# A cross-interaction tower on one core: layer-1 slices cut by samples, G in the same chunk without the DRAM trip, and the weights turned in another order

## The reference

```python
e = jnp.stack([tbl_0[ids[:, 0]], ..., tbl_38[ids[:, 38]]], axis=1)      # (1024, 39, 16)
def _cin_layer(X0, Xi, W, b):
    Wr = W.reshape(H, F0_, Fi)
    return jnp.einsum('hjk,bjd,bkd->bhd', Wr, X0, Xi) + b[None, :, None]
X0 = embedded_features
Xi = X0
for W, b in Ws:                       # three layers
    Xi = _cin_layer(X0, Xi, W, b)
    res.append(Xi.sum(axis=2))        # z0, z1, z2: 128 numbers a sample each
h = jnp.concatenate([z, dense_ctx], axis=1)
h = jnp.maximum(h @ W_top1 + b_top1, 0.0)
h = jnp.maximum(h @ W_top2 + b_top2, 0.0)
y = h @ W_top3
```

## Time and profile before

| what | us |
|---|---|
| median of three runs | 1378.81 |
| lowest and highest run | 1375.5, 1385.89 |
| span of the profiled execution | 1393.5 |
| first layer-1 matmul starts at | 125.98 |
| step 7 of layer 1 starts at | 1209.68 |
| layer 1 ends about | 1354.2 |

### The profile page before, as it was taken

The page is one execution under the profiler, slowest core; times in us unless marked ns, Lnnn a source line. Parts: engine busy times, 40 slices in busy tenths (PEclk is TensorE's granted clock), DMA queues, the critical chain, the costliest instruction groups (busy, mean ns, idle before and its releaser), DMA issues.

```text
span 1393.5 us, 23236 instructions
## 1 busy us (share of the span) xinstructions
PE 1272.0 (91%) x6037; PEld 1041.9 (75%) x6037; DVE 1087.9 (78%) x2694; ACT 1039.8 (75%) x3353; POOL 882.6 (63%) x654
## 2 busy tenths in 40 slices
PE   2127999999999999999999999999999999999997
PEld 2115778777888878787887878787888888887876
DVE  3125898988888788888888888888888888988992
ACT  1114888888788887788777877888778887788772
POOL 6572777786776867686776877686776745363000
PEclk7556999999999999999999999999999999999999
DMA  4042522242233221242223221242232221240000
GB/s 147 10 107 56 139 63 62 75 99 52 62 75 89 57 58 48 68 100 52 65 72 82 57 67 48 68 96 56 56 81 78 58 64 46 65 98 25 16 16 16
DMA packets 71598, 92.39 MB, mean 66 GB/s; under 512 B 31745, under 2 KB 53762, under 8 KB 70306
## 3 DMA queue, kind: packets, MB, share of 16 engines
q1 hardware_dynamic: 61318, 87.75, 24.5%
q0 software_dynamic: 9984, 2.58, 2.0%
q10 hardware_dynamic: 156, 0.48, 0.1%
HBM read 21.03 MB, written 10.95 MB: 23 GB/s over the span
## 4 chain that ended last, share of the span: by engine, by line
PE 81%; DVE 5%; ACT 4%; another core or an unknown queue 4%; issue 4%; DMA 1%; ACTq 0%; POOL 0%; DVEq 0%; SPq 0%; POOLq 0%
PE ring L1098 19%; PE ring L1100 19%; PE ring L1099 18%; PE side L998 4%; PE side L1065 4%; PE l_ps L984 4%; PE l_ps L986 3%; PE l_ps L985 3%; ACT terms L692 2%; DVE x_s L852 2%; DVE terms L897 2%; PE side L1017 1%; PE side L1048 1%; PE side L1026 1%
## 5 line engine op out<-in xcount | busy, mean ns | idle before, releaser
L692 ACT ACTIVATE terms<-ring,e_both 128x128 f32<-128x128 f32 x2944 | 839.2, 403 | 214.4 <-PE ring L1100 180.2
L1098 PE MATMUL ring<-w_hi,x_hi 128*128 128x512 f32 (+1 forms) x1280 | 556.5, 435 | 15.8 <-ACT terms L692 8.7
L897 DVE SCALAR_TENSOR_TENSOR terms<-ring,e_both,terms 128x128 f32<-128x128 f32 x1792 | 507.9, 344 | 65.2 <-PE ring L1100 57.3
L1100 PE MATMUL ring<-w_hi,x_lo 128*128 128x512 f32 (+1 forms) x1280 | 499.1, 390 | 0.0
L1099 PE MATMUL ring<-w_lo,x_hi 128*128 128x512 f32 (+1 forms) x1280 | 497.2, 388 | 0.0
L852 DVE TENSOR_REDUCE x_s<-terms 128x32 f32<-128x800 f32 x512 | 489.1, 976 | 0.7 <-ACT terms L692 0.7
L500 POOL TENSOR_TENSOR pairs_lo<-pairs,pairs_hi 117x1024 fp32r<-117x1024 f32 (+1 forms) x104 | 250.1, 2404 | 231.7 <-ACT pairs_hi L603 226.7
L458 POOL DMA_INDIRECT e_in<-in_tbl,idx x312 | 302.1, 968 | 93.8 <-issue 70.6
L1098 PEld LDWEIGHTS ring<-w_hi,x_hi 128*128 128x128 f32 x1280 | 242.9, 190 | 74.4 <-ACT terms L692 17.7
L1100 PEld LDWEIGHTS ring<-w_hi,x_lo 128*128 128x128 f32 x1280 | 241.1, 188 | 50.5
L489 POOL TENSOR_TENSOR pairs<-x_rep,pairs 117x1024 f32<-117x1024 f32 (+1 forms) x104 | 250.3, 2406 | 36.4 <-DMA pairs<-x_t 35.4
(11 more groups left out here) (113 smaller groups left out, 655.8 us busy)
## 6 DMA issues: line engine op xcount, KB each, us to landing
pairs<-x_t SPq DMA_DIRECT2D x312, 156.0 KB
x_scratch<-x_s SPq DMA_DIRECT2D x32, 256.0 KB, 2.2
x_r<-x_scratch SPq DMA_DIRECT2D x7, 1024.0 KB
x_rep<-x_t SPq DMA_DIRECT2D x45, 156.0 KB
e_in<-in_tbl,idx POOLq DMA_INDIRECT x312
x_scratch<-e_both SPq DMA_DIRECT2D x8, 312.0 KB, 7.6
g_t<-in_L_rec_W SPq DMA_DIRECT2D x1, 2496.0 KB, 15.9
xb<-x_scratch SPq DMA_DIRECT2D x8, 312.0 KB
```

Source lines behind the costliest of these rows:

```text
L692: last = nc.scalar.activation(term(d, ACT_BEFORE[d][g] + i), twos(ring[:, (GROUPS * d + g) % RING, i * H:(i + 1) * H]), ACT.Copy, scale=sc ...
L897: nc.vector.scalar_tensor_tensor(out=acc, in0=y, scalar=scale_of(j, d), in1=acc, op0=ALU.mult, op1=ALU.add).then_inc(dve_unit, 1)
L1098: nc.tensor.matmul(acc, x1_hi[:, x], w1_hi[:, w], start=True, stop=False)
L1100: nc.tensor.matmul(acc, x1_lo[:, x], w1_hi[:, w], start=False, stop=True).then_inc(y_group, 1)
```

## The change

A layer-1 slice now is 8 samples with their 16 columns. It is what a G matmul needs, so `sum_terms` writes a slice of x2 straight to `x2_r` and G of slice r runs in the same step, at the new `G_AT`, without DRAM. For this `x0_t` and x1 have sample-major columns (ScalarE writes `x0_t` with a stride of 16 elements), `x0_t` has two slots (partitions 0 and 64 up), and the scales come from `xb`, X0 by samples and columns, which is written to DRAM and read back a chunk ahead in two slots. All G of a chunk use one bank, so each waits for the evacuation of the one before. z2, the network's three layers and y of a chunk all run in the next step, slices 2 to 9, where g_t is free before its next G. `copy_x0`, the two halves of z0 with their add on GpSimd, and the x2 DMAs are gone. `move_x0` is one turning copy at (2, 5); X0's four transposes follow one at a time through one bank.

In the setup six batches of W1 are turned before step -1 (`W1_EARLY`). The other four and all of W2, which is loaded at the start into `terms`, are turned at (6, 0) of step -1, behind X0's transposes. In step -1 33 gathers for chunk 1 follow (`INDEX_SLICE` 4), and VectorE makes the product of the next tile before the rest of the last.

```diff
-    X0T_AT, X0T_OUT_AT, X0T_BANK = ((5, 0), (5, 2), (8, 9), (9, 9)), ((5, 3), (5, 5), (9, 3), (10, 3)), (1, 0, 1, 1)
+    X0T_AT, X0T_OUT_AT = ((3, 2), (3, 7), (4, 2), (4, 7)), ((3, 5), (4, 0), (4, 5), (5, 0))
+    Z2_PLACES = [(d, g) for d in range(2, 6) for g in range(GROUPS)][1:1 + FIELDS]
+    G_AT = ((6, 5), (6, 9), (7, 2), (7, 7), (8, 2), (8, 7), (9, 2), (9, 7), (10, 4), (11, 4), (12, 4), (13, 4), (14, 4),
+            (15, 4), (16, 4), (17, 4))
+    BLOCK_AT = [d - 1 for d, g in G_AT]
+    H1_AT, H1_OUT_AT = ((6, 6), (6, 8), (7, 4), (7, 5)), (7, 8)
+    H2_AT, H2_OUT_AT = ((8, 3), (8, 4)), (8, 8)
+    Y_AT, Y_OUT_AT = (9, 3), (9, 6)
...
-    GATHERS = (3, 3, 2, 2, 0, 2, 4, 2, 3, 2, 3, 2, 3, 2, 4, 2)
-    INDEX_SLICE = 5
+    GATHERS = (3, 3, 0, 0, 2, 2, 5, 2, 2, 2, 3, 2, 3, 2, 5, 3)
+    INDEX_SLICE = 4
...
+    W1_PIECE, W1_FIRST, W1_EARLY = 2, 2, 6
+    W1_REST_AT = (6, 0)
...
-            return e_mid[:, j, d:d + 1] if d < CUR_FROM else e_cur[:, d, j:j + 1]
+            return xb[:, odd, d, j:j + 1]
...
+            sp.dma_start(w2_raw, W2).then_inc(w2_in, 16)
...
+                    nc.scalar.activation(
+                        x0_t(1 - odd).rearrange("p (b d) -> p d b", d=D)[:, 4 * q:4 * q + 4, :],
+                        side[0:WRAPPED, 0, :].rearrange("p (d b) -> p d b", d=4),
+                        ACT.Copy).then_inc(x0t_ready, 1)
...
+                    nc.vector.tensor_reduce(z0[:, odd, n * half:n * (half + 1)],
+                                            l0_ps[:, :].rearrange("p (b d) -> p b d", d=D),
+                                            AX.X, ALU.add).then_inc(z0_summed, 1)
...
-                        twos(x2_s[:, d % X2_SLOTS, h]),
+                        twos(x2_r[:, d, h]),
...
+                def slice_g(chunk, r):
+
+                    n = SLICES * chunk + r
+                    after(pe, block_made, n + 1)
+                    after(pe, x2_done, n + 1)
+                    after(pe, g_ready, n)
+                    if r == 0:
+                        after(pe, z2_ready, chunk)
+                    nc.tensor.matmul(side[:, 1, 0:SAMPLES * GCOLS], x2_r[:, r, :],
+                                     blocks[:, r % BLOCK_SLOTS, :, :].rearrange("p b j -> p (b j)"),
+                                     start=True, stop=True).then_inc(g_ps, 1)
...
+                    if not layer1 and (d, g) == W1_REST_AT:
+                        for q in range(W1_EARLY, GROUPS):
+                            w1_turned(q)
+                        for q in range(GROUPS):
+                            w2_turned(q)
```

More of the change, by code:

```diff
@@ new lines, in step @@
+                        if not layer1 and i == FIRST_SLOTS - 1:
+                            x0_write()
+                        if i == (0 if layer1 else FIRST_SLOTS):
+                            xb_back()
+                    rep(c + 1, 1, 1 - odd)
+                    pair_tile(c + 1, PAIR_TILES, 1 - odd)
+                if layer1 and not following:
+                    after(sp, dense_ps, c)
+                    sp.dma_start(dense_raw[:, :], dense_ctx[c * P:(c + 1) * P, :]).then_inc(dense_in, 16)
@@ L450, in _ @@
             sp.wait_ge(y_out, 32)
-            for i in range(2):
-                sp.wait_ge(x2_out[i], 32 * CHUNKS)
             sp.wait_ge(x0_out, 16 * CHUNKS)
@@ L470, in _, with step @@
                 gather(0, f)
-            def step(c, odd, layer1, following, previous, mlp, gathers):
+            def step(c, odd, layer1, following, previous, gathers):
                 def next_index():
@@ L564, in _, with step @@
                 last.then_inc(setup_hi, 1)
-            for q in range(W1_FIRST, GROUPS):
+            for q in range(W1_FIRST, W1_EARLY):
                 w1_upper(q)
-            def step(c, odd, layer1, following, previous, mlp, gathers):
+            def step(c, odd, layer1, following, previous, gathers):
                 def x1_half(chunk, half):
@@ new lines, in first_lower @@
+                def first_lower(d):
+                    chunk, i = tile_made(c, d, layer1, following)
+                    n = TILES * chunk + i
+                    rows = ROWS_OF[TILE[i][1]]
+                    after(dve, pair_hi, n + 1)
+                    after(dve, pair_used, n - 1)
+                    nc.vector.tensor_tensor(pairs_lo[0:rows, i % 2, :], pair_slot(chunk, i)[0][0:rows, :],
+                                            pairs_hi[0:rows, i % 2, :].bitcast(f32),
+                                            ALU.subtract).then_inc(pair_lo, 1)
@@ new lines, in first_pairs @@
+                def first_pairs(d, g):
+                    if (d, g) == W1_REST_AT:
+                        for q in range(W1_EARLY, GROUPS):
+                            w1_lower(q)
+                    if g == MADE_MID and tile_made(c, d, layer1, following) and d < D - 1:
+                        first_product(d)
+                        if d > FIRST_MADE:
+                            first_lower(d - 1)
+                    if (d, g) == (FIRST_MADE + PAIR_TILES, 0):
+                        first_lower(d - 1)
+                    if (d, g) == (D - 1, 8):
+                        first_product(d)
+                    if (d, g) == (D - 1, 9):
+                        first_lower(d)
@@ L864, in side_work @@
                             z0_half(half)
-                    if not layer1:
+                    if not layer1 and following:
                         first_pairs(d, g)
@@ L1001, in side_work @@
                             last.then_inc(z2_ps, 1)
+                    if following and (d, g) in X0T_AT:
+                        q = X0T_AT.index((d, g))
+                        if q == 0:
+                            after(pe, e_ready, c + 2)
+                            after(pe, y_ready, c - 1)
+                        else:
+                            after(pe, x0t_ready, 4 * (c + 1) + q)
+                        for i in range(4):
+                            last = nc.tensor.transpose(side[0:TURNED, 0, i * P:(i + 1) * P],
+                                                       e_df[:, 4 * q + i, :], ident[:, :])
+                        last.then_inc(x0t_ps, 1)
                     if previous and (d, g) == DENSE_AT:
```

582 lines of the change are left out of this document (213 added, 369 removed).

## The result

| what | before, us | after, us |
|---|---|---|
| median of the timed runs | 1380.57 (4 runs, 1375.5 to 1385.89) | 1422.74 (4 runs, 1419.8 to 1427.33) |
| span of the profiled execution | 1393.5 | 1420.8 |
| first layer-1 matmul starts | 125.98 | 140.71 |
| eight steps of layer 1 | 1228.2 | 1256.3 |
| from there to the end | 39.3 | 23.8 |

The ratio is 1.0279, with a 95% interval of 1.0224 to 1.0335: the change makes the kernel slower by about 42 us. The forecast was 1365 with a range of 1342 to 1386, so it was wrong in size and in sign.

What follows compares the result with a forecast made beforehand. TensorE's work was taken to bound the middle steps, chains of waits the start and tail. Tail -17.6, layer 1 -2 and start +6 gave -13.6, so 1378.8 became 1365 us, range 1342 to 1386.

Steps and rivals of the forecast that it cites:

- tail -17.6: After the last layer-1 step: z2 no longer waits for x2 from DRAM and starts 17.6 us earlier.
- layer 1 -2: Eight layer-1 steps: steps 2 to 5 save 4 together, step 1 pays +1.7, steps 0 and 7 nothing; together -2 us.
- start +6: Up to the first layer-1 matmul: W1 and W2 batches come late under the gathers, so it starts at 132, +6 us.
- bound of -14: Tail's smallest gain: -14 us if TensorE is half clocked after its 2 us without work.
- Rival D: Tail: the DRAM trip was not what it waited for; tail -12, sum -8, 1371 us; chance 0.10.
- bounds of -10 to +10: Layer 1: -10 us if all waits go but 3.5 us, +10 if light slices 10 to 14 wait for GpSimd.
- rival B: Slices 6 to 9: single bank makes G wait for the evacuation before, +36 us, sum +22, 1401; chance 0.12.
- X0's four parts take 8.6 and are there at 65: Start: X0's transposes and ScalarE's writes, begun at 56.2, take 8.6 us and finish at 65, not late.
- outer bound: Start at its worst: no batch gets through the gathers and X0's parts are late too; first layer-1 matmul at 140, +14 us.
- The sum: Whole kernel: -13.6 us against the profiled span, 1393.5 to about 1379.9; carried to the median, 1365.
- rival A: Start: TensorE's signals are not late under the second run of gathers; start -14 to -18, 1345 us; chance 0.15.
- C: Start eats the tail: X0's parts late and step 0 pays for its G; sum -3, 1376 us; chance 0.13.

Runs made afterwards that it cites:

- Spread: Changed kernel with the gathers of a step spread, three in slice 14 and four in slice 6 in place of five each: 1405.55 us.
- all three edits: Changed kernel with step -1's gathers held until W2's batches are out, the gathers of a step spread, and one G moved to (7, 3): 1385.43 us.
- second profile of before: Kernel before, unchanged, profiled once more: span 1387.4 us, first layer-1 matmul at 120.9.
- long hold: Changed kernel with the second run of gathers, in step -1, held until ScalarE has evacuated all batches of W1 and W2: 1401.7 us.
- plain transfers: Changed kernel with the 33 indirect gathers of step -1 replaced by plain transfers of the same size from GpSimd: 1393.5 us in one run.

## Why the prediction was wrong, point by point

By its own terms, against the profiled span of before: tail -17.6, measured -15.5; layer 1 -2, measured +28.1; start +6, measured +14.7. The measured three add up to +27.3, and 1393.5 + 27.3 = 1420.8.

**The tail** was right in each step. z2 starts 17.1 us earlier, and 1.6 are given back because it runs partly below full clock, which the bound of -14 had allowed for. Rival D, a tail of -12, falls.

**Layer 1** is the step that failed most, outside its bounds of -10 to +10. It was priced by TensorE's work, with 5 us a step as waits of no special cause. The term that is missing is `GATHERS`: the change makes runs of five of the two runs of four, in slices 6 and 14, and slice 14 it has just made light. I had said in the start what a run of gathers does, and did not ask it of the steps, where slices 14 and 15 of the kernel before hint at it: up to 8.9 and 10.3 in steps 2 to 5 (11.6 once), 8.3 and 9.6 in step 6, which has no gathers. Spread, steps 0 to 6 lose 13.6 us, 8 to 15 by the other profiles. The second part is the single bank of rival B: I priced eight places at +36 and gave it 0.12. One place of the sixteen was shown to be caught, (7, 2), at 0.54 a step. Price and mechanism were right, the count was one and not eight; the order of the two lists would have shown it, as ScalarE's evacuation and TensorE's next G stand at the same (7, 2). The third is what is left with all three edits. Step 1 was forecast at +1.7 for the network that it takes over, and is 3.1 over the second profile of before. Steps 2 to 5 were forecast at -4 together and are at +3.7; for these and step 6 the cause stays open. Step 7, forecast at 0, took 2.0 more in the changed kernel, some 0.5 of it at (7, 2), and step 0, also at 0, took 2.5 more than in the first profile of before and 0.9 more than in the second. The prices of single slices held where nothing disturbs: 11.4 in slices 3 and 4 (forecast 11.3), 8.7 to 8.9 in slices 10 to 13 (8.7), 8.9 in slice 15 (9.0).

**The start** had the right mechanism, and the long hold and the plain transfers show it. The step that failed is "X0's four parts take 8.6 and are there at 65": I let the batches be late and left the parts ahead of them on time, except in the outer bound, although show X0's own last part as the one that was late. In one bank four hand-overs stand in a row, each of them late, and the last part is there at 92.3, not at 65. Then none of the fourteen batches got through, where I had counted four; they were free at 103.25, not 101.5. ScalarE's write with a stride of 16 elements was forecast at 1.06 from the turning copy; it took 1.02, and 0.59 without the stride. The Trainium skill (SBUF — State Buffer, Door 1, on SBUF "cachelines") says that each access that crosses to a new 16-byte line pays a penalty; this write agrees.

**The sum** was carried to the median by taking the 14.7 us between span and median off both kernels. That failed too. The 14.7 belonged to that one execution of before, while the changed kernel's profile (1420.8) stands at its own median (1422.7). It is 15 of the 42 us. Where one hand-over is late by 19 us in one execution and 13 in the next, an average start can be earlier than the one in the profile; that the 15 us lie there is argued from three profiles whose starts are 8 us apart, and not shown. The spread of 10 us in three timed runs was there to be read; I used it as an argument for rival A.

**Rivals.** A (nothing late) was the wrong way round. B had a right mechanism at one place. C was the nearest in kind, since the start did eat the tail, but its 1376 lacked the steps.

## What to carry to other kernels

A run of indirect gathers has a price on engines that do not gather: count the hand-overs from TensorE that lie under it, in the start and in every slice, and put the gathers where none is pending, in short runs. A chain that hands over through one bank pays that price at every link, as X0's four parts did; whether two banks would have halved it no run tried. And before a difference of two spans is carried to a median, ask which stretch of the profiled execution differs from run to run.

## What was not expected of the hardware

Four transposes of X0 were taken by ScalarE 6.2 to 10.1 us after their recorded start under a run of indirect gathers, and 1.1 to 1.2 us after it without (56.11 and 57.23 with the long hold). Whether the matmuls themselves ended late or only the news of them, these rows do not tell. The other direction, from ScalarE to TensorE, was not late in any of these rows. Thirty-three plain transfers from the same engine, on the same queue, 0.53 us apiece, held up nothing; thirty-three indirect ones of 1.25 us cost 29 us. With four banks between the engines a run of three gathers in slice 14 is absorbed (8.9 to 9.1 us), and one of five often is not: in steps 2 to 5 of the changed kernel the slice took 10.4 to 11.4, and the slice behind it up to 13.8; in steps 0 and 1 the same five cost nothing.
